# Source indices of a graph gather widened on GpSimd one column behind each gather, in place of 64 columns at once

## The reference

```
xn = layernorm(x)
g  = gcn(relu(gcn(xn, W1, b1)), W2, b2)      # two graph convolutions, 256 -> 128 -> 256
x  = x + g + mix(xn)                         # mix: a linear attention over all nodes
x  = x + ffn(layernorm(x))                   # a feed-forward layer for the nodes that a router selects

def gcn(h, W, b):
    h = h @ W
    s, d = [src, loops], [dst, loops]
    msg = h[s] * (dinv[s] * dinv[d])[:, None]
    return segment_sum(msg, d) + b
```

## Time and profile before

| | |
|---|---|
| runs | 5218.92, 5220.01 and 5222.76 us, median 5220.01 us |
| span of the profiled execution, first to last instruction | 5161.8 us |
| outside the span, against the median | 58.2 us |
| busy: PE, PEld, DVE, ACT, POOL | 52%, 46%, 30%, 21%, 62% |
| layer 1's gathers | 176.3 to about 2551 us of the span |
| layer 2's gathers | 2566.9 to about 5028 us |

### The profile page before, as it was taken

How to read it: one execution, slowest core, us unless ns; L and a number is a source line. 1 busy time by engine, 2 the same in 40 slices (tenths; PEclk the granted TensorE clock), 3 DMA queues, 4 the chain that set the end, 5 groups by cost and what they waited for, 6 DMA issues and landing times.

```text
span 5161.8 us, 57909 instructions
## 1 busy us (share of the span) xinstructions
PE 2699.7 (52%) x15958; PEld 2372.1 (46%) x15959; DVE 1565.2 (30%) x4025; ACT 1070.7 (21%) x2222; POOL 3192.6 (62%) x3394
## 2 busy tenths in 40 slices
PE   6543434434443434333347656656666666665663
PEld 6433333333333333333336555555656555564563
DVE  7222222222222222222223323323333333332336
ACT  2310111101111011110013323323323332332332
POOL 0466666666666666666566666666666666666660
PEclk9766666666666666666668878878888888887886
DMA  4211111111111111111211111111111111111116
GB/s 134 74 48 50 47 48 50 47 49 49 48 49 48 50 48 49 48 48 50 61 48 49 50 48 50 49 47 50 50 50 50 50 49 49 49 51 47 49 49 203
DMA packets 191219, 288.41 MB, mean 56 GB/s; under 512 B 59532, under 2 KB 137524, under 8 KB 190934
## 3 DMA queue, kind: packets, MB, share of 16 engines
q0 software_dynamic: 106304, 217.92, 16.2%
q1 hardware_dynamic: 80868, 65.79, 4.1%
q10 hardware_dynamic: 3968, 3.80, 0.2%
HBM read 248.80 MB, written 38.49 MB: 56 GB/s over the span
## 4 chain that ended last, share of the span: by engine, by line
another core or an unknown queue 44%; PE 22%; issue 14%; ACT 8%; DVE 7%; DVEq 3%; ACTq 0%; DMA 0%; POOL 0%; SPq 0%; POOLq 0%
PE bank L928 8%; PE bank L784 5%; ACT arena L633 3%; PE bank L913 3%; ACT L623 2%; PE bank L911 2%; DVE arena L1226 1%; PE bank L831 1%; PE bank L920 1%; ACT arena L623 1%; DVE acc L1237 1%; DVEq L360 1%; DVEq L1237 1%; DVE arena L1110 1%
## 5 line engine op out<-in xcount | busy, mean ns | idle before, releaser
L516 POOL DMA_INDIRECT arena<-table,indices x3322 | 3173.1, 955 | 1814.7 <-issue 932.8
L784 PE MATMUL bank<-arena 128*128 128x128 f32 x6644 | 1165.9, 323 | 463.8 <-issue 235.0
L784 PEld LDWEIGHTS bank<-arena 128*128 128x128 f32 x6644 | 1104.5, 237 | 536.0 <-issue 299.6
L1237 DVE SCALAR_TENSOR_TENSOR acc<-bank,folded,acc 128x128 f32 x832 | 253.4, 346 | 2568.7 <-remote 2350.0
L1226 DVE SCALAR_TENSOR_TENSOR arena<-indices,base_col,bank 128x1024 f32 (+1 forms) x416 | 532.5, 1280 | 126.8 <-DVE acc L1237 62.4
L940 PE MATMUL bank<-arena 128*128 128x256 f32 x1568 | 401.5, 401 | 162.4 <-ACT arena L633 162.3
L928 PE MATMUL bank<-arena 128*128 128x128 f32 x3136 | 407.6, 285 | 63.4 <-ACT arena L629 35.8
L928 PEld LDWEIGHTS bank<-arena 128*128 128x128 f32 x3136 | 380.2, 198 | 81.3 <-ACT arena L629 47.9
L940 PEld LDWEIGHTS bank<-arena 128*128 128x128 f32 x1568 | 294.8, 198 | 214.3 <-ACT arena L633 179.4
L911 PE MATMUL bank<-folded,arena 128*128 128x256 f32 x196 | 117.3, 702 | 463.0 <-ACT arena L623 458.7
L814 PE MATMUL bank<-arena 128*128 128x256 f32 x392 | 172.6, 589 | 314.8 <-ACT arena L595 222.4
(11 more groups left out here) (256 smaller groups left out, 2351.3 us busy)
## 6 DMA issues: line engine op xcount, KB each, us to landing
arena<-table,indices POOLq DMA_INDIRECT x3322
base_rows<-arena SPq DMA_DIRECT2D x98, 128.0 KB
xs<-in_x_dram SPq DMA_DIRECT2D x6, 1792.0 KB, 16.9
table<-acc SPq DMA_DIRECT2D x98, 64.0 KB
acc<-base_rows SPq DMA_DIRECT2D x7, 896.0 KB, 11.6
out_dram<-acc SPq DMA_DIRECT2D x7, 896.0 KB, 5.0
table<-acc SPq DMA_DIRECT2D x6, 896.0 KB, 4.6
arena<-base_rows SPq DMA_DIRECT2D x5, 896.0 KB, 9.5
```

The costliest lines, as they stand in the source:

```text
L516: pool.indirect_dma_start(ring[:, quarter * HALF + k, :], None, table[layer], bass.IndirectOffsetOnAxis(ap=idx_now[:, gg % 2, c:c + 1], ax ...
L784: last = nc.tensor.matmul(visit_sum[h][:, 0:F], S[:, h, k, :], ring[:, quarter * HALF + k, :], start=(k == 0), stop=(k == chunks - 1))
L1237: last = dve.scalar_tensor_tensor(a, visit_sum[h][:, 0:F], mask[:, ds(turn, 1)], a, ALU.mult, ALU.add)
```

## The change

`next_indices`, which widened a whole set in one cast, becomes `widen`, which widens the columns from `first` to `past`. Ahead of each layer it still widens all 64 columns of set 0. Within a layer the one cast behind the second pair of a set is gone; instead a cast of one column stands behind each gather: behind the gather of column `c` of set gg, column `c` of set gg + 1 is widened. `s_idx` now counts columns, so the wait at the head of a set is for 64 per set. Nothing is computed differently.

```diff
             sets = PAIRS // SETS
-
-            def next_indices(gg):
-                pool.tensor_copy(idx_now[:, gg % 2, :], src_idx[:, gg * SETS * PAIR:(gg + 1) * SETS * PAIR])\
-                    .then_inc(s_idx, 1)
+            per_set = SETS * PAIR
+
+            def widen(gg, first, past):
+                pool.tensor_copy(idx_now[:, gg % 2, first:past],
+                                 src_idx[:, gg * per_set + first:gg * per_set + past]).then_inc(s_idx, past - first)
 
             def gather_layer(layer):
                 for gg in range(sets):
-                    pool.wait_ge(s_idx, layer * sets + gg + 1)
+                    pool.wait_ge(s_idx, (layer * sets + gg + 1) * per_set)
                     for i in range(SETS):
                         for h in range(2):
                             pool.wait_ge(s_sum[layer][h], gg * SETS + i + 1)
...
                                     ring[:, quarter * HALF + k, :], None, table[layer],
                                     bass.IndirectOffsetOnAxis(ap=idx_now[:, gg % 2, c:c + 1], axis=0),
                                 ).then_inc(s_gath[quarter][k // 2], 16)
-                        if i == 1 and gg + 1 < sets:
-                            next_indices(gg + 1)
+                                if gg + 1 < sets:
+                                    widen(gg + 1, c, c + 1)
 
             pool.wait_ge(s_eTe, 2 * (PAIR // 4))
-            next_indices(0)
+            widen(0, 0, per_set)
             pool.wait_ge(s_tab1, 16 * len(TABLE1_PARTS))
             gather_layer(0)
-            next_indices(0)
+            widen(0, 0, per_set)
             pool.wait_ge(s_tab2, 16 * TILES)
             gather_layer(1)
```

## The result

On the chip of the first comparison the changed kernel took 5255.39 us (5253.18 to 5258.90) against 5221.39 us for the kernel before (5218.92 to 5223.41), four runs each: ratio 1.0064 [1.0052, 1.0076], 34 us slower. The forecast was +150 us.

What follows compares the result with a forecast made beforehand. No engine was full; GpSimd was taken as the pacer, with stops following its own runs. Layer 2's 98, layer 1's 53 and 2 for the index wait, less 3 for removed casts, gave 5220 + 150 = 5370 us; range 5090 to 5550.

Steps and rivals of the forecast that it cites:

- The cost of a cast: GpSimd's step from gather to gather: each added one-column cast lengthens it by 0.07 us, from 1.26 to 1.33.
- The exposed share: GpSimd's queue: casts in front of a stop cost nothing, so about 2920 of the 3200 added casts cost time.
- the 53 that were counted: Layer 1: 1600 x 0.95 x 0.07 = 106 us, half counted because part likely comes off a stop.
- counted at 98 us: Layer 2: one cast in eight hidden, runs of 8 locked to their stop, 1600 x 7/8 x 0.07 us.
- a lock: Layer 2: runs of 8 gathers locked to their stop, which follows GpSimd's own end; 182 stops, mean 2.2 us.
- the one that I put under the rival: Evidence for absorbed: runs of 8, 16 and 24 gathers have stops of 1.96, 3.10 and 4.28 us.
- Absorbed: GpSimd's waits: added issue comes off them, price 0 to 40 us, 5210 to 5260 us; chance 0.30.
- Faster: Dense gathers freeze the other engines; more room per gather shrinks or removes stops, 5090 us; chance 0.20.
- The port: Casts and VectorE's two-SBUF-input instructions delay each other: 25 us layer 2, 8 us layer 1; 5253 us alone, chance 0.05.

Runs made afterwards that it cites:

- the second chip: Changed kernel, unaltered, against the kernel before on another chip that also has stops: 5247.12 us against 5168.09, ratio 1.0133 [1.0110, 1.0156].

## Why the prediction was right or wrong

**The cost of a cast was right.** 0.07 us was taken from the removed cast and two fills; the step is 1.33 us as forecast. In the queue that is never stopped the change costs 251 us, 0.078 a cast.

**The exposed share was the step that failed.** "About 2920 of the 3200 are exposed" followed from "The stop thus hangs on when GpSimd's run ended more than on what the other engines have to do". In layer 1 it doesn't: with longer steps the stops fell by as much as was added, and 1600 casts there cost 6 us, with an interval that holds 0, in place of the 53 that were counted. In layer 2, counted at 98 us, the second chip gave some 73 (79 less those 6; 104 in the one trace). That this is near to the forecast's term is luck. The term rests on stops that stay some 2 us long behind runs of 8, and they fell from 1.96 to 1.21 us; the cost came in by long stops behind runs of 16. Of the +34 us of the first comparison the split isn't known; if layer 1 costs 6 us there too, some 28 are left for layer 2.

The rows that I read as a lock, runs of 8 with like stops, fit a cycle of the other engines as well, 11.78 us and then 11.79 on one chip, whatever part of it GpSimd issues in. The row that pointed to it is the one that I put under the rival: in layer 1 the longer run has the longer stop (3.05 us on the mean behind 16 gathers, 4.30 behind 24). A wait that grows with what lies before it can be slack that an addition comes out of.

**The rivals.** *Absorbed* is what happened in layer 1 and in layer 2's runs of 8; its 5210 to 5260 us hold the 5255 measured, and the stops' sum fell by about the 200 us that it named. It isn't the whole of it: its 0 to 40 us would give 5168 to 5208 us on the second chip, where 5247 were measured, and runs of 16 with long stops aren't in it. *Faster* fell: stops went from 260 to 239 in the two stretches, and they shrank by no more than the steps had grown. *The port* is there. Timeline of all engines in layer 2, changed kernel:

```profile
3366.47 0.42 DVE L1422 TENSOR_TENSOR arena<-arena 128x256 f32<-128x256 f32 x1 [0.94 <-issue]
3366.51 0.43 POOL L504 CAST indices<-indices 128x1 int32<-128x1 int16 x1
3366.93 0.42 DVE L1424 CUSTOM_DVE_ANT_0 arena<-arena,folded 128x256 f32<-128x256 f32 x1
```

A cast that begins 0.04 us into a VectorE instruction with two SBUF inputs takes 0.43 us in place of 0.20 and ends 0.05 us behind it. Counted over the whole trace, 145 casts took over 0.24 us, by 24 us in sum, 23 in layer 2 and 1 in layer 1; the prediction had 25 and 8. All 84 casts that began within line 1422 are among them, with 18 of the 24 us, and none of the 380 that began within line 1227, 1.28 us long, whose second tensor input lies in PSUM. Two SBUF inputs aren't the whole condition: 42 of the 145 began within lines 1401 and 1416, with one each (4 us). VectorE loses nothing: its line 1404 (1403 of before) has 425 ns and its line 1276 (1275 of before) 354, against the earlier trace rows. The Trainium skill's page "SBUF — State Buffer" (Who interferes with whom) says that a VectorE instruction with two SBUF inputs contends with a GpSimd instruction that reads SBUF. The trace agrees for line 1422, with the loss on GpSimd's side alone. What these 24 us did to the time isn't shown. On the second chip, with 23 us of them, they can't be all of the cost, and the runs of 8 took them in too; in the first comparison they are of the size of what layer 2 may have cost, and no run tells them apart from it.

**What stays open.** Why the kernel has some 280 stops on two chips and none on four isn't settled. Each chip was used at one time only, so chip and time aren't told apart. No line of the kernel differs, and the gathers' DMA packets take as long in sum at both levels (16.2% of 5161.8 us and 18.6% of 4492.2, 836 us each). What the other engines need without stops (at most 10.2 us a pair in layer 1, 16.8 in layer 2) is far below the 22.9 and 23.7 us of a pair with them, so their work by itself doesn't explain the stops. The clock was higher there, 0.95 and 0.89 against 0.65 and 0.83; if all of that work went by it, an estimate from these numbers, the needs would be 14.9 and 18.0 us, still far below. Whether fewer gathers, fewer bytes or fewer products would shorten a pair at that level wasn't tried there.

One thing goes with the level in all twenty traces: how many changes of semaphores they hold. Each gather's landing adds 16 to its semaphore, one at a time, 53,152 for 3322 gathers. The twelve traces without stops and with all gathers hold 53,006 or more of them, the three with half of the gathers 26,841 to 26,843 of 26,848; the five with stops hold 12,733 to 16,513. So "remote" and "another core or an unknown queue", 44 to 45% of the chain, are in those five best read as missing records, not as a sender elsewhere, and the traces without stops show no "remote": by the program, a stop of GpSimd in front of a gather is a wait for TensorE's sum (line 511), apart from the wait at the head of a set. Whether what drops these records also holds the engines up, so that the slower level belongs to the recording and not to the kernel, is a rival that no run here tests.

## What to carry to other kernels

A small instruction put behind each step of a queue costs what it takes beyond the issue time that is there anyway (here 0.075 of 0.20 us, the next one 0.11), and 64 columns cost little more than one: widen 64 columns at once. Whether that reaches the end depends on whether the queue ever waits; where a stop grows with the run in front of it, part or all of the addition can come off it, and a run with the addition in one layer alone tells how much. Before setting a profile beside other runs, see that its execution took as long as they did, and that both are of one chip. And before reading "remote" as another sender, count whether the trace holds the releases at all.

## What was not expected of the hardware

- The same program ran at 4492 to 4503 us on four chips and at 5168 and 5221 us on two, a step of 15%, and the granted clock doesn't explain it (0.725 in the trace of before without stops, 0.745 and 0.746 in the two with them). The price of the change went with it: +251 us against +79 and +34.
- Two casts in a row overlap: the second starts 0.13 us behind the first, which takes 0.19.
- A gather behind a cast takes 0.97 us in place of 0.95, and the added instructions bring fetches with them: one queue of instruction loads (q14) had 49 packets before and 74 after, 25 more for 3150 instructions of GpSimd, the only engine whose program grew.
